# Moving the node numbers of the first edge stage's 0/1 matrices from SBUF into PSUM

## The chip, the core and the metric

The program runs on one core of a Trainium2 chip. The metric is the device time of one execution in microseconds (us). Three executions of the kernel before took 6554.74, 6558.20 and 6558.29 us, median 6558.2 us.

The engines are named as the profile names them: PE (TensorE matmul; PEld its weight loads), DVE (VectorE), ACT (ScalarE), POOL (GpSimd) and SP (SyncE, which issues DMAs here). SBUF is the working memory that all of them reach; PSUM holds the matmuls' outputs, in eight banks of 512 four-byte numbers per partition.

## The reference, cut to what matters

Two layers, each a graph attention followed by a mixture-of-experts feed-forward, over 6250 nodes with 256 features and 206250 edges sorted by their destination. The change lies in the attention of the first layer:

```
h = (x @ W.T).reshape(n, H, D)                        # H = 8 heads, D = 32
alpha = einsum(h[src], a_src) + einsum(h[dst], a_dst) + sum(relu(edge_attr @ edge_W.T + edge_b) * h[dst])
alpha = where(alpha >= 0, alpha, 0.2 * alpha)
ex = exp(alpha - segment_max(alpha, dst)[dst])
attn = ex / maximum(segment_sum(ex, dst)[dst], 1e-10)
out = segment_sum(h[src] * attn[..., None], dst) + bias
```

## The kernel before, in words

`edge_phase` runs once per layer. Edges go through it in groups of 512 (`G`), each group as 4 chunks (`CH`) of 128 edges on the 128 partitions. A group's destinations lie in a window of 32 nodes (`WIN`). Thirteen groups (`SB`) make a batch; 31 batches make a stage. Two batches stand in double buffers: `k` is 0 or 1 in `rows[:, k]`, `oh[:, k]`, `sel[:, k]` and `ps_w[:, k]`, where each `k` of `ps_w` is one PSUM bank. A loop body (`Fori`) holds two batches.

The engines work a batch in program order, tied by semaphores:

- POOL does nothing but `gather` (L774): 52 indirect DMAs per batch, each fetching the 128 source rows of a chunk from HBM by the numbers in `eidx`. Four gathers of batch b+2, slot s, may start when PE has finished slot s of batch b (`s_o`).
- PE, in slot s of batch b: `total` (L880, L886) sums the weighted rows of the 4 chunks into the window's 32 nodes, with the 0/1 matrix `oh` as weights, and carries the part that belongs to the window before with the 0/1 matrix `sel`. Between these it computes for batch b+2 the encodings (L809, L811) and scores (L821) of the edges. In slot 1 it adds the source logits of batch b+1 (`logits`, L851), which ACT copies out of the fetched rows (`sources`, L950) once all 52 gathers of that batch have landed; in slot 10 it writes batch b+1's transposed softmax weights into bank `1-k` of `ps_w` (L870), in columns 0 to 103 of each chunk's 128.
- ACT takes its work in this order: evict slot s (L973), the two ReLUs of batch b+2 (L946), and in slot 1 `sources` behind them.
- DVE scales the fetched rows by the weights (L1141), writes 0/1 matrices of owners (L1064), multiplies encodings (L1073), and once per batch does the maxima (L1094, L1099, L1103), a short chain on one partition (L1106 to L1118), `peaks` (L1122 to L1128) and, in slot 9, `one_hots` (L1085 and L1088).

`one_hots` for batch b+1 compares every edge's distance `dn` (SBUF, 52 numbers per partition) with the numbers 0 to 31 and so writes 52 x 32 = 1664 elements of `oh`; a second instruction does the same for `sel` (416 elements). In the first layer both tables of numbers lie in SBUF (`miota`, `pm`); in the second layer they are copied at the start into a PSUM bank of their own (`ps_i`), which the first layer has no room for.

At the stage's start DVE clears buffers and then increments `s_ready`; SP waits for that before it loads the first index tables, and POOL for the tables before its first gather.

Of the kernel before, what the change touches and what calls it, by code (L numbers as in the profile page):

```python
# [10 lines left out]
ALU = mybir.AluOpType  # L11
# [3 lines left out]
P = 128  # L15
# [8 lines left out]
CH = G // P  # L24
# [5 lines left out]
WIN = 32  # L30
K3 = 3 * WIN
SB = 13
COLS = SB * HEADS
# [33 lines left out]
def hold(eng, sem, value, passed):  # L67


    eng.wait_ge(sem, value)  # L70
    eng.sem_inc(passed, 1)
# [478 lines left out]
def edge_phase(nc, io, dr, layer):  # L550

    first = layer == 0
    with ExitStack() as ctx:
# [3 lines left out]
        OHW = SB * CH * WIN  # L557
# [10 lines left out]
        miota = sb("miota", [P, WIN], F32)  # L568
        pm = sb("pm", [P, WIN], F32)
# [3 lines left out]
        dn = sb("dn", [P, SB, CH], F32)  # L573
        dd = sb("dd", [P, SB], F32)
        oh = sb("oh", [P, 2, OHW + PAD_M], F32)
# [21 lines left out]
        if first:  # L597
            hp = sb("hp", [K3, RING, D], BF16)
            w_st = sb("w_st", [4, D], F32)
            w_rest = sb("w_rest", [4, D], F32)  # L600
            w_part = sb("w_part", [4, 3, D], BF16)
            w_enc = sb("w_enc", [K3, D], BF16)
            adst = sb("adst", [P, 2], F32)
            hmask = sb("hmask", [P, 2, HEADS], F32)
            hwide = sb("hwide", [P, 2, WIDE], F32)
            encr = sb("encr", [P, 2, G], F32)
            u = sb("u", [P, 2, 2, G], F32)
            lk, fmax, near = sb("lk", [COLS, G], F32), sb("fmax", [COLS, G], F32), mx
            nodes, lags = miota, pm
            ps_enc = ps("ps_enc", [P, 2, 512])  # L610
            ps_hd = ps("ps_hd", [P, 2, 512])
        else:
            aw = sb("aw", [K3, RING, WIDE], BF16)
            ps_k, ps_f, ps_i = ps("ps_k", [P, 512]), ps("ps_f", [P, 512]), ps("ps_i", [P, 512])
            lk, fmax, near = ps_k[0:COLS, :], ps_f[0:COLS, :], ps_f[0:COLS, :]
            nodes, lags = ps_i[:, 0:WIN], ps_i[:, WIN:2 * WIN]
        ps_X = ps("ps_X", [P, 512])
        ps_o = ps("ps_o", [P, OB, 512])
        ps_w = ps("ps_w", [P, 2, CH, P])
        small = lambda k: ps_w[:, k, :, :].rearrange("p j c -> p (j c)")  # L620
        s_nb, s_const, s_w, s_wp, s_we, s_init, s_ready = (sem(n) for n in ("nb", "const", "w", "wp", "we", "init", "ready"))
        s_ld = [sem(f"ld{r}") for r in range(RING)]
# [35 lines left out]
        def _(sp):  # L658
# [8 lines left out]
            def entry(t):  # L667
                why = "the planning stage writes only groups and starts of windows that lie inside their arrays"
                _, vals = nc.values_load_multi_w_load_instructions(tab[0:1, bass.ds(t * 3, 3)], engines=[sp.engine], min_val=0, max_val=NP,
                                                                   skip_runtime_bounds_check_because=why)  # L670
                return [nc.s_assert_within(x, 0, NG - 1 if c == 0 else NP, skip_runtime_bounds_check_because=why) for c, x in enumerate(vals)]
# [70 lines left out]
            for j in range(BEHIND):  # L742
                t = steps * (2 * SB) + (3 * SB + j)
                _, _, back = entry(t)
                store(t, j % SB, back)
# [270 lines left out]
        def _(v):  # L1016
            steps = [0]

            def done(ins):

                steps[0] += 1
                ins.then_inc(s_init, 1)
                v.wait_ge(s_init, steps[0])
# [13 lines left out]
            if first:  # L1037
                done(nc.vector.memset(hwide[:, :, :], 0.0))
                done(nc.vector.memset(w_enc[:, :], 0.0))
                done(nc.vector.tensor_copy(hwide[:, :, COLS - HEADS:COLS], hmask[:, :, :]))  # L1040
                v.sem_inc(s_ready, 1)
                v.wait_ge(s_w, 48)
                done(nc.vector.tensor_copy(w_part[:, 0, :], w_st[:, :]))
                done(nc.vector.tensor_tensor(w_rest[:, :], w_st[:, :], w_part[:, 0, :], ALU.subtract))
                done(nc.vector.tensor_copy(w_part[:, 1, :], w_rest[:, :]))
                done(nc.vector.tensor_tensor(w_rest[:, :], w_rest[:, :], w_part[:, 1, :], ALU.subtract))
                nc.vector.tensor_copy(w_part[:, 2, :], w_rest[:, :]).then_inc(s_wp, 1)
            else:
                done(nc.vector.memset(aw[:, :, :], 0.0))
                done(nc.vector.tensor_copy(nodes, miota[:, :]))  # L1050
                done(nc.vector.tensor_copy(lags, pm[:, :]))
                v.sem_inc(s_ready, 1)

# [28 lines left out]

            def one_hots(b, k):
                hold(v, s_dn, b * 2 + 2, s_pv)
                nc.vector.tensor_tensor(oh[:, k, 0:OHW].rearrange("p (x m) -> p x m", m=WIN),  # L1085
                                        dn[:, :, :].rearrange("p s j -> p (s j)").unsqueeze(2).to_broadcast([P, SB * CH, WIN]),
                                        nodes[:, :].unsqueeze(1).to_broadcast([P, SB * CH, WIN]), ALU.is_equal)
                nc.vector.tensor_tensor(sel[:, k, 0:SELW].rearrange("p (x m) -> p x m", m=WIN),  # L1088
                                        dd[:, :].unsqueeze(2).to_broadcast([P, SB, WIN]),
                                        lags[:, :].unsqueeze(1).to_broadcast([P, SB, WIN]), ALU.is_equal)  # L1090
# [54 lines left out]
            def phase(b, k, pre, turn, turns, next_turns):  # L1145
                m, n = b + 1, b + 2
                if pre:
                    node_ids(n, k, next_turns)
                if first and pre:
                    owners(n, k, 0, par(0))  # L1150
                carried(b, k)
                for s in range(SB):
                    if s + 2 < SB:
                        scaled(b, k, s + 2)
                    elif turn:
                        scaled(m, 1 - k, s + 2 - SB)
                    if pre and s + ahead < SB:
                        owners(n, k, s + ahead, par(s + ahead))
                    if first and pre:
                        products(n, s, par(s))  # L1160
                    if turn and s == 0:
                        distances(m, 1 - k, turns)
                    if turn and s == 1:
                        largest(m)
                    if turn and s == 2:
                        runs_forth(m, 1 - k, turns)
                    if turn and s == 3:
                        runs_back(m, 1 - k)
                    if turn and s == 5:
                        chain(m, 1 - k)  # L1170
                    if turn and s == 8:
                        peaks(m, 1 - k)
                    if turn and s == 9:
                        one_hots(m, 1 - k)
# [3 lines left out]
            for s in range(SB):  # L1178
                if s + 1 < SB:
                    owners(0, 0, s + 1, (s + 1) % 2)  # L1180
                if first:
                    products(0, s, s % 2)
            distances(0, 0, 0)
            one_hots(0, 0)
            largest(0)
            runs_forth(0, 0, 0)
# [600 lines left out]
def build(nc, io, out):  # L1787
    dr = scratch(nc)
    plan_phase(nc, io, dr)
    node_phase(nc, io, dr, 0)  # L1790
    edge_phase(nc, io, dr, 0)
    ffn_phases(nc, io, dr, 0, io["x"], dr["x2"], dr["x2"])
    node_phase(nc, io, dr, 1)
    edge_phase(nc, io, dr, 1)
    ffn_phases(nc, io, dr, 1, dr["x2"], dr["x3"], out)
# [22 lines left out]
```

## Time and profile before

| | |
|---|---|
| three executions | 6554.74, 6558.20, 6558.29 us |
| the profiled execution | 6560.36 us, span 6558.6 us (1.8 us lie outside the span) |
| PE busy | 4742.2 us, 72% of the span |
| POOL busy | 3639.3 us, 55% |
| DVE busy | 3265.5 us, 50% |
| ACT busy | 1360.8 us, 21% |
| first edge stage, first to last gather | 242.6 to 2341.3 us |
| second edge stage, first to last gather | 3739.3 to 5775.3 us |

Times count from the span's start. A row of the timeline gives the start, the duration, the engine, the line of the kernel, the operation, what it writes and reads, how many like it are merged, and in brackets how long the engine stood idle before it and what ended that. "issue" there is idle time that no semaphore explains. `e_` stands before the names of both edge stages. Matmuls are pipelined and their ends modelled, so PE's busy time says that work was in it, not that it ran at its peak.

### The profile page before, as it was taken

Reading aid. Unit: us, or ns where it says so; the run is one execution under the profiler, and the core shown is the slowest. Engines: PE = TensorE matmul, PEld = TensorE weight load, DVE = VectorE, ACT = ScalarE, POOL = GpSimd, SP = SyncE. Lnnn points to the kernel's source line nnn. Section 1 sums busy time; section 2 is a strip of 40 time slices with the busy share of each in tenths; the row PEclk is TensorE's granted clock in tenths of the full one; section 3 lists DMA queues with packets and bytes.
Section 4 is the critical chain, followed back from the end, with each engine's and each line's share of the span. In section 5 each row is a group of like instructions: output and inputs, shape, how many; then the busy total and the mean of one; then the engine's idle time right before and its main releaser. Section 6 shows DMA issues by size and latency. Waiting matters only on the chain. (4 is left out here: it accounts for less than half of the span.)

```text
span 6558.6 us, 98463 instructions
## 1 busy us (share of the span) xinstructions
PE 4742.2 (72%) x19729; PEld 3561.5 (54%) x19729; DVE 3265.5 (50%) x5938; ACT 1360.8 (21%) x2977; POOL 3639.3 (55%) x3708
## 2 busy tenths in 40 slices
PE   1699999999999963099999436565656565643798
PEld 0355555555555543099999325444544444433698
DVE  6666767767777757111111334444444444454344
ACT  1333333333333311022222201010101010101122
POOL 1677777777777720512222177777777777711322
PEclk9899999999999995599999668788888887875899
DMA  6566666666666634256666455555555555542455
GB/s 219 180 172 164 163 164 162 163 165 165 163 165 166 160 94 170 87 177 183 185 185 185 134 133 141 140 139 141 139 141 139 140 139 140 138 131 103 176 199 184
DMA packets 718012, 1022.22 MB, mean 156 GB/s; under 512 B 301733, under 2 KB 531561, under 8 KB 692608
## 3 DMA queue, kind: packets, MB, share of 16 engines
q0 software_dynamic: 183456, 485.95, 28.5%
q1 hardware_dynamic: 527676, 519.31, 25.9%
q10 hardware_dynamic: 6564, 14.14, 0.6%
q14 instruction: 287, 2.35, 0.1%
q8 instruction: 29, 0.48, 0.0%
HBM read 868.26 MB, written 153.27 MB: 156 GB/s over the span
## 5 line engine op out<-in xcount | busy, mean ns | idle before, releaser
L774 POOL DMA_INDIRECT e_rows<-sc_table,e_eidx x3224 | 3141.4, 974 | 1007.1 <-issue 932.1
L880 PE MATMUL e_ps_o<-e_rows,e_oh 128*128 128x264 f32 x6448 | 1633.5, 398 | 53.2 <-DVE e_rows L1141 26.9
L880 PEld LDWEIGHTS e_ps_o<-e_rows,e_oh 128*128 128x128 f32 x6448 | 1230.0, 195 | 412.8 <-issue 214.0
L1141 DVE TENSOR_TENSOR e_rows<-e_rows,e_ps_w 128x1024 f32<-128x1024 f32 x806 | 969.7, 1206 | 13.2 <-issue 9.6
L1073 DVE SCALAR_TENSOR_TENSOR e_u<-e_encr,e_adst,e_ps_hd 128x512 f32<-128x512 f32 x806 | 588.1, 743 | 470.8 <-PE e_ps_X L821 391.0
L821 PE MATMUL e_ps_X<-e_u,e_hwide 128*104 128x512 f32 x1612 | 806.3, 593 | 0.0
L973 ACT COPY e_res<-e_ps_o 32x264 f32<-32x264 f32 x806 | 296.4, 368 | 2131.1 <-PE e_ps_o L886 1689.5
L851 PE MATMUL e_ps_X<-e_ident,e_alog 128*104 128x128 f32 x496 | 97.9, 361 | 828.1 <-ACT e_alog L950 828.1
L1685 PE MATMUL x_ps_h<-x_xT,x_w 128*128 128x256 f32 x2624 | 647.2, 405 | 14.6 <-DMA x_b<-in_L_ffn_b_dram 14.6
L1685 PEld LDWEIGHTS x_ps_h<-x_xT,x_w 128*128 128x128 f32 x2624 | 638.0, 337 | 19.3 <-issue 15.5
L1696 PE MATMUL x_ps_y<-x_w,x_hT 128*128 128x256 f32 x2624 | 579.9, 379 | 0.0
L851 PEld LDWEIGHTS e_ps_X<-e_ident,e_alog 128*104 128x104 f32 x496 | 82.6, 234 | 854.9 <-issue 854.9
L1655 POOL DMA_INDIRECT sc_x<-x_y,x_idx x108 | 168.0, 1555 | 665.8 <-DVE x_idx L1729 649.2
L1696 PEld LDWEIGHTS x_ps_y<-x_w,x_hT 128*128 128x128 f32 x2624 | 492.9, 190 | 63.5
L946 ACT ACTIVATE e_encr<-e_ps_enc 128x512 f32<-128x512 f32 x806 | 468.9, 588 | 241.8 <-PE e_ps_enc L809 232.3
L1708 ACT ACTIVATE x_hT<-x_ps_h,x_b 128x256 f32<-128x256 f32 x656 | 305.4, 474 | 780.3 <-PE x_ps_h L1685 779.5
L886 PE MATMUL e_ps_o<-e_res,e_sel 128*128 128x264 f32 x1488 | 456.2, 389 | 0.0
L1064 DVE TENSOR_SCALAR e_ohT<-e_at,e_nid 96x512 bf16<-96x512 int16 x806 | 296.0, 368 | 319.9 <-DMA e_aw<-sc_a2p 213.7
L1094 DVE TENSOR_TENSOR e_ps_k<-e_ps_X,e_y 104x512 f32<-104x512 f32 x31 | 21.7, 699 | 820.8 <-ACT e_y L954 820.8
L821 PEld LDWEIGHTS e_ps_X<-e_u,e_hwide 128*104 128x104 f32 x1612 | 273.9, 170 | 179.5 <-issue 65.5
L1350 POOL DMA_INDIRECT sc_xb<-r_xt,r_slot_i x98 | 95.0, 969 | 437.2 <-DVEq L1555 407.9
L809 PE MATMUL e_ps_enc<-e_at,e_w_enc 96*128 96x512 bf16 x806 | 309.3, 384 | 38.8 <-DMA e_w_enc<-e_w_part 35.9
(290 smaller groups left out, 4066.7 us busy)
## 6 DMA issues: line engine op xcount, KB each, us to landing
x_w<-in_L_ffn_W_dram SPq DMA_DIRECT2D x112, 1024.0 KB
e_at<-sc_grp SPq DMA_DIRECT2D x403, 192.0 KB
x_w<-in_L_ffn_w_dram SPq DMA_DIRECT2D x60, 1024.0 KB
e_rows<-sc_table,e_eidx POOLq DMA_INDIRECT x3224
e_at<-sc_grp SPq DMA_DIRECT2D x403, 96.0 KB
sc_agg<-e_res SPq DMA_DIRECT2D x816, 33.0 KB
sc_xb<-r_zero SPq DMA_DIRECT2D x24, 1032.0 KB
x_xin<-sc_xb SPq DMA_DIRECT2D x86, 258.0 KB
```

What stands on the lines that cost most here:

```text
L774: pool.indirect_dma_start(rows[:, k, s, j, :], None, dr["table"][:, :], bass.IndirectOffsetOnAxis(eidx[:, k, s, j:j + 1], 0)).then_inc(s_r ...
L809: nc.tensor.matmul(ps_enc[:, h, :], w_enc[:, h * P:(h + 1) * P], at[:, ring(s), 0, :].bitcast(BF16), start=True, stop=True).then_inc(s_enc, 1)
L821: nc.tensor.matmul(ps_X[0:COLS, :], hwide[:, h, COLS - HEADS * (s + 1):2 * COLS - HEADS * (s + 1)], u[:, par(s), h, :], start=(s == 0 and ...
L880: nc.tensor.matmul(ps_o[:, q, 0:ROW], oh[:, k, at_j:at_j + P], rows[:, k, s, j, :], start=(j == 0), stop=False)
L886: nc.tensor.matmul(ps_o[:, q, 0:ROW], sel[:, k, s * WIN:s * WIN + P], seen, start=False, stop=True).then_inc(s_o, 1)
L946: nc.scalar.activation(encr[:, h, :], ps_enc[:, h, :], ACT.Relu).then_inc(s_relu, 1)
L973: nc.scalar.copy(res[0:WIN, kept(s), :], ps_o[0:WIN, par(s) % OB, 0:ROW]).then_inc(s_ev, 1)
L1073: nc.vector.scalar_tensor_tensor(u[:, p, h, :], encr[:, h, :], adst[:, h:h + 1], ps_hd[:, h, :], ALU.add, ALU.mult).then_inc(s_u, 1)
L1141: nc.vector.tensor_tensor(part, part, ps_w[:, k, :, s * HEADS:(s + 1) * HEADS].unsqueeze(3).to_broadcast([P, CH, HEADS, DH]), ALU.mult).th ...
L1685: mm = nc.tensor.matmul(ps_h[:, j % 4, 0:TB], w1[:, k, c, :].rearrange("p (m j) -> p j m", j=FC)[:, j, :], xT[:, k, c, :], start=(c == 0), ...
L1696: mm = nc.tensor.matmul(ps_y[:, s, 0:D], hT[:, k, j, s * P:(s + 1) * P], w2[:, k, j, :], start=(j == 0), stop=(j == FC - 1))
L1708: nc.scalar.activation(hT[:, k, j, :], ps_h[:, j % 4, 0:TB], ACT.Gelu if first else ACT.Relu, bias=b1[:, k, j:j + 1]).then_inc(s_act, 1)
```

## The change

The lag table `pm` stays where it was. The node numbers of the first layer get a second home: columns 104 to 119 of two of the four chunks of each `ps_w` bank, which the transposed weights (columns 0 to 103) and the small results in chunk 0 and chunk 3 leave alone. Sixteen numbers stand in each piece, so that both layers' comparison now walks its 32 columns as 2 x 16. For batch b+1 with buffer `1-k`, the numbers are read from bank `k`, the one that PE and ACT are not about to write for batch b+1. The second layer's table stays in `ps_i` and is only walked in the new way.

```
-            nodes, lags = miota, pm
+            lags = pm
...
-            nodes, lags = ps_i[:, 0:WIN], ps_i[:, WIN:2 * WIN]
+            lags = ps_i[:, WIN:2 * WIN]
...
+        HALF = WIN // 2
+        halves = lambda tile: tile.rearrange("p (a m) -> p a m", m=HALF)
+        nodes = (lambda k: ps_w[:, k, 1:3, COLS:COLS + HALF]) if first else (lambda k: halves(ps_i[:, 0:WIN]))
...
                 done(nc.vector.tensor_copy(hwide[:, :, COLS - HEADS:COLS], hmask[:, :, :]))
+                for k in range(2):
+                    done(nc.vector.tensor_copy(nodes(k), halves(miota[:, :])))
                 v.sem_inc(s_ready, 1)
...
-                done(nc.vector.tensor_copy(nodes, miota[:, :]))
+                done(nc.vector.tensor_copy(nodes(0), halves(miota[:, :])))
...
-                nc.vector.tensor_tensor(oh[:, k, 0:OHW].rearrange("p (x m) -> p x m", m=WIN),
-                                        dn[:, :, :].rearrange("p s j -> p (s j)").unsqueeze(2).to_broadcast([P, SB * CH, WIN]),
-                                        nodes[:, :].unsqueeze(1).to_broadcast([P, SB * CH, WIN]), ALU.is_equal)
+                nc.vector.tensor_tensor(oh[:, k, 0:OHW].rearrange("p (x a m) -> p x a m", a=2, m=HALF),
+                                        dn[:, :, :].rearrange("p s j -> p (s j)").unsqueeze(2).unsqueeze(3).to_broadcast([P, SB * CH, 2, HALF]),
+                                        nodes(1 - k).unsqueeze(1).to_broadcast([P, SB * CH, 2, HALF]), ALU.is_equal)
```

DVE's program at the start of the first edge stage before (`e_hwide` and `e_w_enc` are weights of the encoding, `e_w_st` and `e_w_part` its inputs being split):

```order
L1039 MEMSET e_w_enc 96x128
L1040 COPY e_hwide<-e_hmask 128x2x8
L1043 CAST e_w_part<-e_w_st 4x256
L1044 TENSOR_TENSOR e_w_rest<-e_w_st,e_w_part 4x256
L1045 CAST e_w_part<-e_w_rest 4x256
```

The same place in the changed kernel:

```order
L1042 MEMSET e_w_enc 96x128
L1043 COPY e_hwide<-e_hmask 128x2x8
L1045 COPY e_ps_w<-e_miota 128x2x16 x2
L1048 CAST e_w_part<-e_w_st 4x256
L1049 TENSOR_TENSOR e_w_rest<-e_w_st,e_w_part 4x256
```

Two copies have come in between the last copy and the increment of `s_ready`; nothing else moved on this engine.

DVE's program around the 0/1 matrices in the loop body before (L70 rows are register work of the waits):

```order
L1073 SCALAR_TENSOR_TENSOR e_u<-e_encr,e_adst,e_ps_hd 128x512
L1085 TENSOR_TENSOR e_oh<-e_dn,e_miota 128x1664
L1088 TENSOR_TENSOR e_sel<-e_dd,e_pm 128x416
L1141 TENSOR_TENSOR e_rows<-e_rows,e_ps_w 128x4x256
L70 ISA
L1064 TENSOR_SCALAR e_ohT<-e_at,e_nid 96x512
```

And in the changed kernel:

```order
L1078 SCALAR_TENSOR_TENSOR e_u<-e_encr,e_adst,e_ps_hd 128x512
L1090 TENSOR_TENSOR e_oh<-e_dn,e_ps_w 128x1664
L1093 TENSOR_TENSOR e_sel<-e_dd,e_pm 128x416
L1146 TENSOR_TENSOR e_rows<-e_rows,e_ps_w 128x4x256
L70 ISA
L1069 TENSOR_SCALAR e_ohT<-e_at,e_nid 96x512
```

The order is the same; the second input of the larger comparison is now `e_ps_w` instead of `e_miota`. The programs of PE, ACT, POOL and SP are as they were.

## Rows read from the trace of the kernel before

**Rows 1.** Windows: us, then busy of PE, PEld, DVE, ACT, POOL; clock; DMA; both stages.
```profile
242.60:2341.30 2098.70, 1989.79 (x7609) 1203.07 (x7610) 1450.64 (x2193) 639.33 (x1335) 1604.47 (x1612) 0.98 0.61 164
3739.00:5776.00 2037.00, 1121.71 (x4793) 877.43 (x4793) 884.82 (x1387) 212.22 (x530) 1536.93 (x1612) 0.79 0.55 139
```

**Rows 2.** Groups of POOL, first stage, then second.
```profile
L774 POOL DMA_INDIRECT e_rows<-sc_table,e_eidx x1612 | 1604.5, 995 | 500.8 <-issue 457.7 <-PE e_ps_o L886 36.5 <-DMA e_eidx<-sc_eslot 6.6
...
L774 POOL DMA_INDIRECT e_rows<-sc_table,e_eidx x1612 | 1536.9, 953 | 506.3 <-issue 474.4 <-PE e_ps_o L886 24.7 <-DMA e_eidx<-sc_eslot 7.3
```

**Rows 3.** Timeline, POOL and DVE around one pair of comparisons, first stage.
```profile
1034.29 2.26 POOL L774 DMA_INDIRECT e_rows<-sc_table,e_eidx  x1 [0.30 <-PE e_ps_o L886]
...
1033.35 1.88 DVE L1085 TENSOR_TENSOR e_oh<-e_dn,e_miota 128x1664 f32<-128x1664 f32 x1
1035.15 0.58 DVE L1088 TENSOR_TENSOR e_sel<-e_dd,e_pm 128x416 f32<-128x416 f32 x1
```

**Rows 4.** Timeline, the same place in the second stage.
```profile
4097.28 0.95 POOL L774 DMA_INDIRECT e_rows<-sc_table,e_eidx  x1 [0.30 <-issue]
...
4096.30 1.88 DVE L1085 TENSOR_TENSOR e_oh<-e_dn,e_ps_i 128x1664 f32<-128x1664 f32 x1
```

**Rows 5.** L1085: count, ns min/median/max, first and last start; by form.
```profile
L1085 DVE TENSOR_TENSOR e_oh<-e_dn,e_miota x31: 1874/1877/1892, 301.2 to 2368.7; 128x1664 f32<-128x1664 f32 x31
L1085 DVE TENSOR_TENSOR e_oh<-e_dn,e_ps_i x31: 1871/1877/1886, 3769.8 to 5799.6; 128x1664 f32<-128x1664 f32 x31
```

**Rows 6.** Groups of ACT from 445 to 2345 us: `sources`.
```profile
L950 ACT COPY e_alog<-e_rows 128x416 f32<-128x416 f32 x29 | 15.2, 523 | 2.8 <-DMA e_rows<-sc_table,e_eidx 2.8
```

**Rows 7.** Timeline, PE's `logits` in one batch, ACT's `sources` in another.
```profile
1057.77 1.09 PE L851 MATMUL e_ps_X<-e_ident,e_alog 128*104 128x128 f32 x8 [1.31 <-ACT e_alog L950]
...
1193.17 0.54 ACT L950 COPY e_alog<-e_rows 128x416 f32<-128x416 f32 x1 [1.32 <-DMA e_rows<-sc_table,e_eidx]
```

**Rows 8.** Timeline of PE behind two such waits, and the window of the first.
```profile
1194.78 3.63 PE L880 MATMUL e_ps_o<-e_rows,e_oh 128*128 128x264 f32 x8
...
1736.66 1.95 PE L880 MATMUL e_ps_o<-e_rows,e_oh 128*128 128x264 f32 x8
...
1194.82:1198.24 3.42, 3.42 (x10) 2.61 (x9) 2.08 (x3) 0.60 (x1) 2.51 (x4) 0.50 0.58 177
```

**Rows 9.** Timeline, DVE: the larger comparison of the next three batches.
```profile
1100.05 1.88 DVE L1085 TENSOR_TENSOR e_oh<-e_dn,e_miota 128x1664 f32<-128x1664 f32 x1
...
1168.00 1.88 DVE L1085 TENSOR_TENSOR e_oh<-e_dn,e_miota 128x1664 f32<-128x1664 f32 x1
...
1237.70 1.87 DVE L1085 TENSOR_TENSOR e_oh<-e_dn,e_miota 128x1664 f32<-128x1664 f32 x1
```

**Rows 10.** Timeline, the edge of the loop body: DVE and PE.
```profile
1117.93 0.23 DVE L1056 TENSOR_SCALAR e_nid<-e_ns,e_q 96x13 f32<-96x13 f32 x1 [3.65 <-issue]
...
1119.62 0.68 PE L886 MATMUL e_ps_o<-e_cs,e_sel 128*128 128x264 f32 x2 [1.01 <-DVE e_cs L1135]
```

**Rows 11.** Timeline, the stage's start: DVE, SP, POOL, ACT.
```profile
239.59 0.17 DVE L1040 COPY e_hwide<-e_hmask 128x16 f32<-128x16 f32 x1
...
239.85 0.40 SPq L675 DMA_DIRECT2D e_eidx<-sc_eslot  x1
...
302.06 1.82 POOL L774 DMA_INDIRECT e_rows<-sc_table,e_eidx  x1 [0.30 <-issue]
...
378.73 0.54 ACT L950 COPY e_alog<-e_rows 128x416 f32<-128x416 f32 x1 [3.71 <-DMA e_rows<-sc_table,e_eidx]
```

**Rows 12.** L1051, the second stage's table copy: count, ns, start.
```profile
L1051 DVE COPY e_ps_i<-e_pm x1: 195/195/195, 3736.2 to 3736.2; 128x32 f32<-128x32 f32 x1
```

**Rows 13.** L1108: count, ns min/median/max; timeline, POOL beside L1128, DVE behind a pair.
```profile
L1108 DVE COPY e_qrow<-e_ps_w x62: 514/524/534, 318.6 to 5788.6; 1x208 f32<-1x208 f32 x62
...
1030.29 1.19 POOL L774 DMA_INDIRECT e_rows<-sc_table,e_eidx  x1 [0.30 <-issue]
...
1040.86 0.75 DVE L1073 SCALAR_TENSOR_TENSOR e_u<-e_encr,e_adst,e_ps_hd 128x512 f32<-128x512 f32 x1 [1.03 <-PE e_ps_X L821]
```

## The prediction

> **What bounds the kernel now.** I read four views of the first edge stage, since the change acts only there: the windows, the groups of POOL, the timeline around one pair of comparisons, and who ends ACT's and PE's waits.
>
> The windows show a stage of 2098.70 us between first and last gather, with matmuls in 1989.79 us of it and POOL busy for 1604.47 us [rows 1]. The groups of POOL show that the rest of POOL's time is not waiting for anybody: 1612 gathers of 995 ns with about 0.30 us between them [rows 2]. Busy plus idle is 1604.5 + 500.8 = 2105.3 us, the whole stage and the wait before its first gather. So POOL runs back to back, 2098.7 / 31 = 67.70 us per batch, and looks like the bound.
>
> It is slowed in this stage. A gather that comes up against DVE's two comparisons takes 2.26 us instead of 0.95 [rows 3]: the comparison starts at 1033.35, the smaller one ends at 1035.73, and the gather ends 0.82 us later. In the second stage the same comparison, with its second input in PSUM, runs over a gather of 0.95 us [rows 4], and the mean gather there is 953 ns against 995 [rows 2]. The two stages differ by 1604.5 - 1536.9 = 67.6 us of POOL time; the pair of comparisons accounts for (2.26 - 0.95) x 30 = 39 us of it.
>
> But who waits for POOL? ACT's `sources` needs all 52 gathers of a batch. From 445 us to the end of the stage, 29 batches, ACT stood idle for them 2.8 us in all [rows 6]. In a usual batch ACT goes from its ReLUs straight to the copy, and PE waits 1.31 us for that chain [rows 7], which no gather shortens. Between one comparison and the next lie 66.70 us (1033.35 to 1100.05), then 67.95 us [rows 3, 9]. The longer ones hold the loop's edge, where DVE is idle 3.65 us with no cause that a semaphore shows and PE waits 1.01 us for DVE's carried sums [rows 10]. So PE sets the pace, and POOL keeps up with almost nothing to spare.
>
> **The larger comparison.** 31 instructions in each stage, 1664 elements as before. Its duration with the second input in PSUM is in the trace: 1877 ns median, against 1877 with both inputs in SBUF [rows 5]. What no row shows is runs of 16 numbers with a gap between them. From below I take no gain. From above I take the PSUM copy with short runs, 208 elements in 524 ns [rows 13], against the table copy, 32 elements in 195 ns [rows 12]: 329 / 176 = 1.87 ns per element, where the two comparisons cost (1877 - 580) / (1664 - 416) = 1.04 ns [rows 3, 5]. That would add 0.83 x 1664 = 1.4 us. I take 0, because the same instruction is the nearest row. If it came, 1.03 us of it lie beside idle DVE time, for behind the pair DVE next waits 1.03 us for PE [rows 13].
>
> The Trainium skill (VectorE: DVE Perf Modes, section on the TRN2 errata) gives a VectorE operation from PSUM a fixed 120 cycles where one from SBUF has 58, 62 cycles at 0.96 GHz or 0.065 us. By that, an estimate from the page, the stage's comparisons would cost 31 x 0.065 = 2.0 us more on DVE; by the two equal medians [rows 5] they cost nothing, and the measurement decides.
>
> **POOL's stall.** Removed: the part of the 1.31 us that the larger comparison causes. Left: the smaller one, 0.58 us with both inputs in SBUF [rows 3]. Its residue is between 0 (a gather is past its start) and 0.58 us; I take 0.24, from the gather of 1.19 us beside the subtraction L1128, which also has two inputs in SBUF and ends the batch's `peaks` [rows 13]. So POOL saves 1.31 - 0.24 = 1.07 us per batch, between 0.73 and 1.31, and its pace becomes 67.70 - 1.07 = 66.6 us, below PE's mean, which is (66.70 + 67.95) / 2 = 67.3 us for the pair shown. POOL then runs ahead until it waits for `s_o`; that wait holds nobody, since the gathers are a batch and more ahead of their use.
>
> **What this gives the stage.** Only where somebody waited for gathers.
> 1. The three waits of 1.32, 0.92 and 0.53 us that make up the 2.8 us: -2.8 us [rows 6, 7].
> 2. Behind the first of them the clock is granted at half for 3.42 us, at 0.50 that is 1.2 GHz, after PE had stood idle; eight matmuls took 3.63 us there and 1.95 in the batch of the second wait [rows 8]. The batch took 1237.70 - 1168.00 = 69.70 us; less 66.70, less the 1.4 us of wait, 1.6 us remain for the clock: -1.6 us. Bounds 0 (the low clock comes elsewhere) and -1.7 from the matmuls.
> 3. The start. ACT waited 3.71 us for batch 1's gathers at 378.73 [rows 11], so everything behind follows POOL there. The gather beside the first comparison took 1.82 us, 0.87 too long, with some 0.1 left to the smaller comparison: -0.8 us.
> 4. Added: two table copies, each waited for, between L1040 and `s_ready`. SP issues the index table 0.09 us behind L1040's end, so it waited for DVE [rows 11]. The second stage's copy takes 0.195 us and its neighbour starts 0.23 us earlier, so 2 x 0.23 = +0.5 us, bounds 0.3 and 0.6.
>
> The sum is -2.8 - 1.6 - 0.8 + 0.5 = -4.7 us. Against the profiled execution: 6560.4 - 4.7 = 6555.7 us. That execution was 2.2 us above the median of the three runs, 6558.2, so I forecast 6553.5 us.
>
> The second stage: POOL is as busy as before, its comparison never held a gather, and the new walk through the same table is the question bounded above. DVE is busy 884.82 of 2037 us there [rows 1], which hides 31 x 1.4 us too. I take 0. After the stage nothing is changed.
>
> **Rivals.**
> A. POOL sets the pace. For it: POOL never pauses, and its 67.70 us equal the stage's own pace. Then all of the relief arrives: 30 x 1.07 + 0.8 - 0.5 = 32 us, or 6526 us; with the full 1.31 us, 39 us. Against it: 2.8 us of waiting in 29 batches, and a batch of 66.70 us while POOL needs 67.70 on average. What speaks for a part of it is that POOL drops back until it causes a wait now and then; that part is in my sum.
>
> B. The stall stays, because it hangs on something else than two inputs in SBUF (the table's place is not what holds the gather, or the smaller comparison holds it all). Only the copies remain: +0.5, or 6558.7 us. Against it stands the second stage, where the gather under the comparison took 0.95 us [rows 4]. The Trainium skill (SBUF — State Buffer, section on its two separate sides) says that a VectorE operation with two SBUF inputs and a GpSimd operation exclude each other for a whole instruction; by that rule, the trace agrees that the larger comparison stops holding gathers and the smaller one does not.
>
> C. Slower: the walk in runs of 16 from PSUM lengthens the comparison, and DVE's slack behind it is not there. It sits at L1085's place in both stages. With 1.4 us per batch and 1.03 covered it costs 31 x 0.37 = 11 us; with nothing covered 31 x 1.4 = 43 us, less the 4.7 gained: 6597 us. It decides from about 1.6 us of added length where the cover holds, since (1.6 - 1.03) x 31 = 18 us outweighs the 4.7 by 13. Against it: L1085's equal medians, and DVE's 1450.64 us of 2098.70.
>
> **How the numbers follow.** Forecast 0.79, A 0.12, B 0.05, C 0.04. The forecast's own range is 6548 to 6560 us: nothing gained and the copies paid at the top with a run at the high end, and at the bottom the full sum, the low clocks of two more batches saved (1.6 us each, as behind the first wait), and a run at the low end of the three. For 8 in 10 with A and C outside, the range is 6544 to 6561 us. Within 0.2% of 6558.2, about 13 us and roughly what a measurement of this kernel can tell from no change, lie the forecast and B; with the edges of the forecast that makes 0.83 for no change, 0.13 for faster (A), 0.04 for slower (C).
>
> **What the profile would show.** Right: L1090 with `e_ps_w` at 1.88 us; no gather of 2.26 us, the longest beside the smaller comparison under 1.6 us; POOL busy near 1604.5 - 33 = 1571 us in the stage, with idle time now ended by PE's sums; `sources` waiting for gathers under 1 us behind the first two batches; most distances between comparisons still 66.70 us, those at the loop's edge unchanged. Wrong: distances below 66.5 us (A); gathers still of 2.26 us (B); L1090 above 2.9 us, or PE waiting for DVE in slots 10 and 11 (C). The forecast also fails if the waits at the loop's edge turn out to hang on the gathers, which I have taken as DVE's own.

## The result, and the profile after

The changed kernel is slower: 6580.4 us, median of 6 runs (6574.7 to 6586.7), against 6555.7 us for the kernel before in the same series (6 runs, 6546.7 to 6558.3). The ratio is 1.0039, with a 95% interval of 1.0028 to 1.0050. The forecast was 6553.5 us with 6561 as its upper end, and slower had a chance of 4%. The prediction was wrong.

| profiled execution | before | after |
|---|---|---|
| span | 6558.6 us | 6572.6 us |
| first gather of the first stage | 242.6 us | 244.6 us |
| first edge stage, first to last gather | 2098.7 us | 2117.0 us |
| between the stages | 1398.0 us | 1399.2 us |
| second edge stage | 2036.0 us | 2027.2 us |
| behind it | 783.3 us | 784.6 us |

The loss of 18.3 us stands in the first edge stage, the one that the change was to relieve. (The second stage of the kernel before was some 8 us slow in this one profiled execution, with gathers of 953 ns; in eleven of the twelve other kernels profiled here it took 2026 to 2029 us, with gathers of some 950 ns. Compared by medians the change costs 24.7 us, by profiled executions only 14: beside those 8 us, the profiled execution after, 6574.8 us, is at the low end of its six.)

The two windows after, with the columns of [rows 1] (us, then busy time of PE, PEld, DVE, ACT, POOL, granted clock, DMA share):

```profile
244.60:2361.60 2117.00, 1995.91 (x7604) 1205.95 (x7604) 1448.61 (x2193) 639.64 (x1335) 1558.45 (x1612) 0.98 0.61 162
3760.00:5788.10 2028.10, 1119.66 (x4793) 876.24 (x4793) 883.91 (x1387) 212.16 (x530) 1530.52 (x1612) 0.79 0.56 140
```

POOL is busy 46.0 us less than in [rows 1], more than the 33 us forecast, DVE's busy time has hardly moved (2.0 us less), and PE's has grown by 6.1 us with no more matmuls. So the stage became longer by waiting, for the most part. The group of POOL answers to [rows 2], the timeline beside a pair of comparisons to [rows 3], and the group of ACT's `sources`, from 446 us on, to [rows 6]:

```profile
L777 POOL DMA_INDIRECT e_rows<-sc_table,e_eidx x1612 | 1558.5, 967 | 565.6 <-issue 454.7 <-PE e_ps_o L889 103.8 <-DMA e_eidx<-sc_eslot 7.1
```

```profile
1248.18 0.95 POOL L777 DMA_INDIRECT e_rows<-sc_table,e_eidx  x1 [0.30 <-PE e_ps_o L889]
1249.43 1.01 POOL L777 DMA_INDIRECT e_rows<-sc_table,e_eidx  x1 [0.30 <-issue]
...
1247.24 1.87 DVE L1090 TENSOR_TENSOR e_oh<-e_dn,e_ps_w 128x1664 f32<-128x1664 f32 x1
1249.04 0.57 DVE L1093 TENSOR_TENSOR e_sel<-e_dd,e_pm 128x416 f32<-128x416 f32 x1
```

```profile
L953 ACT COPY e_alog<-e_rows 128x416 f32<-128x416 f32 x29 | 15.1, 521 | 0.0
```

The gather under the comparison takes 0.95 us where it took 2.26, and the next one, beside the smaller comparison, 1.01. Of 1612 gathers 29 were over 2 us before and none is after; the mean has gone from 995 to 967 ns, POOL waits 103.8 us for PE instead of 36.5, and ACT waits for no gather at all. And the comparison that reads PSUM in runs of 16 is no longer than before [rows 5]:

```profile
L1090 DVE TENSOR_TENSOR e_oh<-e_dn,e_ps_w x31: 1868/1872/1889, 304.2 to 2389.7; 128x1664 f32<-128x1664 f32 x31
```

The change did what it says. What became late instead is in PE's waits in the stage (columns: total us, times, longest), here for the kernel before and then for the changed one:

```profile
PE e_ps_X L851 <- ACT e_alog L950: 39.2, 28, 2.7
PE e_ps_o L886 <- DVE e_cs L1135: 18.9, 13, 2.3
```

```profile
PE e_ps_X L854 <- ACT e_alog L953: 40.9, 29, 4.2
PE e_ps_o L889 <- DVE e_cs L1140: 36.1, 13, 3.7
```

PE waits for the carried sums `e_cs` 13 times in either kernel, once at each edge of the loop body, but for 36.1 us instead of 18.9, or 1.32 us longer each time. The distances from one larger comparison to the next say the same: over the 14 even batches from the third on they add up to 937.9 us before and 933.9 after (all at 66.7 after), over the 13 batches with an edge in them to 892.6 and 917.5. So the even batches gained 4.0 us, the 13 edges lost 24.9.

The timeline of DVE and PE at one edge, before (columns: start, duration, engine, line; the idle time ahead and its releaser in brackets):

```profile
1255.52 0.23 DVE L1056 TENSOR_SCALAR e_nid<-e_ns,e_q 96x13 f32<-96x13 f32 x1 [3.58 <-issue]
1256.31 0.39 DVE L1064 TENSOR_SCALAR e_ohT<-e_at,e_nid 96x512 bf16<-96x512 int16 x1 [0.56 <-DVE e_nid L1056]
1256.62 0.40 DVE L1133 TENSOR_TENSOR e_cs<-e_res,e_ps_w 32x256 f32<-32x256 f32 x1
1256.95 0.14 DVE L1135 TENSOR_TENSOR e_cs<-e_res,e_ps_w 32x8 f32<-32x8 f32 x1
1258.02 1.22 DVE L1141 TENSOR_TENSOR e_rows<-e_rows,e_ps_w 128x1024 f32<-128x1024 f32 x1 [0.93 <-issue]
...
1257.23 0.68 PE L886 MATMUL e_ps_o<-e_cs,e_sel 128*128 128x264 f32 x2 [0.98 <-DVE e_cs L1135]
```

And the same edge after:

```profile
1265.31 0.23 DVE L1061 TENSOR_SCALAR e_nid<-e_ns,e_q 96x13 f32<-96x13 f32 x1 [3.83 <-issue]
1266.10 0.35 DVE L1069 TENSOR_SCALAR e_ohT<-e_at,e_nid 96x512 bf16<-96x512 int16 x1 [0.56 <-DVE e_nid L1061]
1267.77 0.41 DVE L1138 TENSOR_TENSOR e_cs<-e_res,e_ps_w 32x256 f32<-32x256 f32 x1 [1.32 <-issue]
1268.11 0.14 DVE L1140 TENSOR_TENSOR e_cs<-e_res,e_ps_w 32x8 f32<-32x8 f32 x1
1268.18 1.20 DVE L1146 TENSOR_TENSOR e_rows<-e_rows,e_ps_w 128x1024 f32<-128x1024 f32 x1
...
1268.39 0.68 PE L889 MATMUL e_ps_o<-e_cs,e_sel 128*128 128x264 f32 x2 [2.60 <-DVE e_cs L1140]
```

DVE halts twice behind the loop's branch in both kernels, and no semaphore ends either halt. The first, of about 4 us, is in the same place. The second stood ahead of L1141, which PE does not wait for at once; it now stands two instructions earlier, ahead of the carried sums, which PE does wait for. Over all 13 edges the groups of DVE give 9.6 us of it before and 19.7 after, 0.74 and 1.52 us an edge (columns as in [rows 6]; before, then after):

```profile
L1141 DVE TENSOR_TENSOR e_rows<-e_rows,e_ps_w 128x1024 f32<-128x1024 f32 x377 | 454.9, 1207 | 9.6 <-issue 9.6
L1138 DVE TENSOR_TENSOR e_cs<-e_res,e_ps_w 32x256 f32<-32x256 f32 x29 | 11.8, 408 | 19.7 <-issue 19.7
```

Counted in the trace with waits and register work, before, the 15th instruction behind the branch meets the second halt, after, the 13th. Two is the number of copies that the change adds to DVE's program, ahead of the loop.

What a longer wait can do to the clock stands at another edge after, in the timeline of PE and the windows of its wait and of what follows:

```profile
1130.62 1.10 PE L889 MATMUL e_ps_o<-e_cs,e_sel 128*128 128x264 f32 x2 [2.42 <-DVE e_cs L1140]
```

```profile
1128.20:1130.60 2.40, 0.00 (x0) 0.01 (x1) 0.95 (x4) 0.00 (x0) 0.95 (x1) 1.00 0.41 113
1130.62:1134.00 3.38, 3.38 (x8) 1.90 (x9) 1.95 (x3) 1.48 (x3) 1.17 (x2) 0.52 0.01 2
```

PE did nothing for 2.4 us, and the 3.38 us behind that ran at a granted clock of 0.52, near the lower level of 1.2 GHz: the same two matmuls took 1.10 us, and 0.68 in the fence above, where a wait of 2.60 us was followed by no such stretch. So the length of one wait does not decide it, but longer waits meet it more often: between 380 and 2330 us there are 7 such stretches after (23.9 us in all), all of them at edges, and 3 before (10.2 us), two of them at edges and the third the one of [rows 8]. At 1.6 us each, the price read from that one in the prediction's second term, four more make 6 us, as much as PE's busy time grew. For the edges alone it is five more, an estimated 8 us, and these with the 17.2 us of longer waits make the 24.9 that the edges lost.

### The profile page after: what moved, and what is told of

It is laid out like the page before. It is cut to its first block and busy times, and to the rows that moved or that the text cites. A ratio compares the mean times of both kernels' runs of the same rounds, so it can differ in the third digit from the quotient of the medians.

```text
span 6572.6 us, 98465 instructions
## 1 busy us (share of the span) xinstructions
PE 4747.4 (72%) x19729; PEld 3564.3 (54%) x19729; DVE 3263.7 (50%) x5940; ACT 1361.0 (21%) x2977; POOL 3585.9 (55%) x3708
## 5 line engine op out<-in xcount | busy, mean ns | idle before, releaser
L777 POOL DMA_INDIRECT e_rows<-sc_table,e_eidx x3224 | 3089.0, 958 | 1069.7 <-issue 925.5
L1690 PEld LDWEIGHTS x_ps_h<-x_xT,x_w 128*128 128x128 f32 x2624 | 637.6, 337 | 19.1 <-issue 15.6
```

The costliest lines, as they stand in the source:

```text
L777: pool.indirect_dma_start(rows[:, k, s, j, :], None, dr["table"][:, :], bass.IndirectOffsetOnAxis(eidx[:, k, s, j:j + 1], 0)).then_inc(s_r ...
L1690: mm = nc.tensor.matmul(ps_h[:, j % 4, 0:TB], w1[:, k, c, :].rearrange("p (m j) -> p j m", j=FC)[:, j, :], xT[:, k, c, :], start=(c == 0), ...
```

## The experiments

The theory: DVE gets its program in pieces. The branch at the loop's edge makes it fetch a piece (first halt), and where that piece ends soon behind the branch's target (the instruction that the branch goes to) it halts again for the next (second halt). Adding instructions ahead of the loop moves the places where pieces end, and two moved the second halt ahead of the carried sums. The rival: the way of the change itself costs the time at the edge, by DVE's reads of the other batch's PSUM bank, or by gathers that now come at other moments. In each series the kernels ran on one chip, with runs of the kernel before beside them; its medians there were 6552.6 us (for the first four kernels of the table), 6549.3 (the next four) and 6550.6 us (the last three). The last two columns come from the one profiled execution of each; there the kernel before has 2098.7 and 18.9 us and the changed kernel 2117.0 and 36.1.

| kernel | median us | ratio to before, interval | first stage us | PE's waits for `e_cs` us |
|---|---|---|---|---|
| pad2_only | 6583.05 | 1.0046 (1.0032 to 1.0059) | 2124.8 | 34.7 |
| psum_unshifted | 6546.43 | 0.9991 (0.9982 to 1.0000) | 2094.7 | 17.9 |
| before_pad13 | 6616.97 | 1.0097 (1.0082 to 1.0113) | 2160.9 | 64.9 |
| before_pad14 | 6579.27 | 1.0041 (1.0027 to 1.0054) | 2115.7 | 34.5 |
| psum_early60 | 6545.65 | 0.9994 (0.9984 to 1.0003) | 2091.4 | 18.3 |
| psum_early100 | 6539.97 | 0.9984 (0.9975 to 0.9994) | 2090.6 | 17.3 |
| psum_early117 | 6542.08 | 0.9991 (0.9981 to 1.0000) | 2087.4 | 16.8 |
| before_early100 | 6550.39 | 1.0001 (0.9991 to 1.0011) | 2100.4 | 15.6 |
| after_early98 | 6545.49 | 0.9996 (0.9987 to 1.0005) | 2085.9 | 15.6 |
| after_carried | 6567.28 | 1.0025 (1.0015 to 1.0035) | 2122.3 | 6.4 |
| psum_early100_carried | 6535.55 | 0.9976 (0.9966 to 0.9986) | 2083.7 | 3.5 |

### The two copies without the change

Into the kernel before, behind L1040; nobody reads what they write:

```diff
+for k in range(2):
+    done(nc.vector.tensor_copy(ps_w[:, k, 1:3, COLS:COLS + WIN // 2], miota[:, :].rearrange("p (a m) -> p a m", m=WIN // 2)))
```

> The kernel before with the two copies of the change added at DVE's start and never read; the comparison still reads its node numbers from SBUF in runs of 32. Theory (place of the code): the two added instructions move everything behind them in DVE's program by two places, so that DVE's second halt at the loop's edge comes ahead of the carried sums (L1133) instead of behind them. Then this kernel is slow too: PE's waits for the carried sums in the first stage add up to 34 to 38 us instead of 18.9, the stage grows by 15 to 20 us, and the time is 6570 to 6580 us. Rival 1 (the PSUM table): reading the numbers from the weights' banks or in runs of 16 costs the time; then this kernel takes 6556 us, within 4. Rival 2 (POOL ahead): gathers that run ahead of PE lengthen DVE's halt at the edge; then too 6556 us, since POOL is held as before here.

It took 6583.05 us, 30.4 above the kernel before and as much as the changed kernel, with its 29 gathers of over 2 us still there. The expectation was 3 us short. The edge is that of the changed kernel:

```profile
1269.36 0.23 DVE L1058 TENSOR_SCALAR e_nid<-e_ns,e_q 96x13 f32<-96x13 f32 x1 [4.11 <-issue]
...
1271.54 0.41 DVE L1135 TENSOR_TENSOR e_cs<-e_res,e_ps_w 32x256 f32<-32x256 f32 x1 [0.82 <-issue]
```

Its waits of PE:

```profile
PE e_ps_o L886 <- DVE e_cs L1137: 34.7, 13, 3.8
```

The whole loss comes with two copies that have nothing to do with the comparison, while the comparison still reads SBUF and the gathers are held as before, so both forms of the rival fall.

### The change without two more instructions

In the changed kernel, one copy for both banks and one clear where there were two, so that DVE's program is as long as before:

```diff
-for k in range(2):
-    done(nc.vector.tensor_copy(nodes(k), halves(miota[:, :])))
+done(nc.vector.tensor_copy(ps_w[:, :, 1:3, COLS:COLS + HALF], halves(miota[:, :]).unsqueeze(1).to_broadcast([P, 2, 2, HALF])))
...
+if first:
+    nc.vector.memset(oh[:, :, OHW:OHW + PAD_M], 0.0)
...
-nc.vector.memset(oh[:, k, OHW:OHW + PAD_M], 0.0)
+if not first:
+    nc.vector.memset(oh[:, k, OHW:OHW + PAD_M], 0.0)
```

> The change whole, but with DVE's program kept at its old length: both banks are filled by one copy, and the clearing of two buffers' ends (L1031) is one instruction instead of two, so everything behind stands where it stood in the kernel before. Theory (place of the code): PE's waits for the carried sums fall back to 17 to 21 us, no gather is over 2 us, and the time is the one first forecast, 6546 to 6554 us, about 5 under before. Rivals 1 and 2 (PSUM table; POOL ahead): as slow as the changed kernel, 6575 to 6585 us.

It took 6546.43 us, 6.2 below the kernel before, inside the expected range. PE's waits for the carried sums are back to 17.9 us, and ACT's for gathers stay at nothing. So the loss is gone once the change does not move the program, and what is left agrees with the 4.7 us of the prediction's sum, though the interval (0 to 12 us) would also admit nothing.

### The end of a piece moved on purpose

Clears of one unused number each, behind L1047 of the kernel before: 13 should let the first piece end just behind the target of the branch, 14 should let a piece begin there.

```diff
+for i in range(13):   # 14 in the other kernel
+    nc.vector.memset(spare[0:1, i:i + 1], 0.0)
```

> The kernel before with 13 clears of one unused number each behind L1047, where DVE waits for a table anyway. Theory (place of the code): 14 of DVE's instructions behind the loop's branch come with the first piece of code now, so with 13 more ahead only one does, and DVE halts a second time ahead of L1056. The carried sums then come about 1.3 us later than in the changed kernel: PE waits for them about 4 us per edge, 52 us in all, and the time is 6585 to 6605 us. Rivals: padding does nothing beyond its 13 x 0.1 us beside a wait, 6556 us.

> As the one with 13, but 14 clears. Theory (place of the code): the first instruction behind the branch is now the first of its piece, so a whole piece is there after the first halt and the second halt disappears: no idle time without a cause ahead of L1141 at the edge, PE waits for the carried sums 15 to 20 us in all, and the time is 6545 to 6556 us, a cliff of 30 us or more against 13 clears. Rivals: no difference between 13 and 14.

With 13 the time is 6616.97 us, 64 above the kernel before and 12 above the expected range, with 64.9 us of waits where 52 were expected; with one clear more it falls by 38 us. The timeline of one edge with 13:

```profile
1285.02 0.23 DVE L1059 TENSOR_SCALAR e_nid<-e_ns,e_q 96x13 f32<-96x13 f32 x1 [7.38 <-issue]
```

Both halts stand one behind the other ahead of L1059. The page's row on the queue of instructions (packets, MB, share), with 13 clears and then before:

```profile
q14 instruction: 300, 2.46, 0.1%
```

```profile
q14 instruction: 287, 2.35, 0.1%
```

Thirteen packets more for thirteen edges, of some 8 KB each (0.11 MB / 13): one fetch more at each edge. The groups of DVE at the first instruction behind the branch (columns as in [rows 6]), with 14 clears and then before:

```profile
L1059 DVE TENSOR_SCALAR e_nid<-e_ns,e_q 96x13 f32<-96x13 f32 x28 | 6.9, 247 | 63.2 <-issue 63.2
```

```profile
L1056 DVE TENSOR_SCALAR e_nid<-e_ns,e_q 96x13 f32<-96x13 f32 x28 | 9.9, 354 | 52.2 <-issue 52.2
```

With 14 the second halt is gone, as expected, but the first is 63.2 / 13 = 4.86 us and not 52.2 / 13 = 4.02, and that was not: the expected 6545 to 6556 us were missed by 23.

The packets of q14 themselves, timed in the traces, show what ends the halts. In the kernel before, at each of the 13 edges one packet lands 2.8 us behind the branch on average and a second at 5.5; DVE's first instruction starts 1.5 to 1.7 us after the first of them, and L1141, behind the second halt, 1.3 to 1.5 us after the second. In the changed kernel the carried sums start 1.1 to 1.5 us after the second. With 13 and with 14 clears two packets stand close together (2.4 and 3.5 us behind the branch with 13, 2.6 and 3.6 with 14), and DVE starts only 1.6 to 1.7 us after the later one. That is the longer first halt, and with 13 a part of the excess over the expectation. Why the engine needs two packets there stays open.

### Long first pieces

If a first piece ends far behind the target, the next has come by then. In `psum_unshifted` and in the kernel before, n clears of an unused number at the end of DVE's part of the planning stage, far ahead of the edge stage:

```diff
+for i in range(100):   # 60 and 117 in the other kernels
+    nc.vector.memset(spare[0:1, i:i + 1], 0.0)
```

> The same with 60 clears: 82 instructions come with the first piece. Theory (place of the code): no halt near the edge but the first; 6538 to 6552 us if that is 4.0 us, 6560 to 6570 if it is 4.9. Rival: 6546.

> The same with 100 clears: 42 instructions behind the branch come with the first piece. Theory (place of the code): as with 117, 6538 to 6552 us if the first halt stays at 4.0 us, 6560 to 6570 if it is 4.9. Rival: 6546.

> The change whole on DVE's old length (one copy for both banks, one clear merged), and 117 clears of one unused number each at the end of the planning stage, where DVE waits 32 us at a barrier. If a piece of DVE's code holds 128 instructions, 25 of them behind the loop's branch now come with the first piece instead of 14. Theory (place of the code): the second halt at the edge moves behind instruction 25, where DVE has other work or is late anyway, so the halt ahead of L1141 (0.8 us per edge) goes; PE's waits for the carried sums stay near 18 us, or rise towards 35 us if the first halt grows by 0.9 us as it did with the branch's target at a piece's start. Time 6538 to 6552 us in the first case, 6560 to 6570 in the second. Rival (only the number of clears right ahead of the stage matters): 6546, as without them.

> The kernel before (numbers in SBUF) with the 100 clears. Theory (place of the code): the change's own worth is the same at every place, 4 to 8 us, so this is 4 to 8 us slower than psum_early100. Rival (the worth hangs on the place): outside that.

The three of the changed way (`psum_early60`, `psum_early100`, `psum_early117`) are inside their expected ranges and within 6 us of each other, at 6545.65, 6539.97 and 6542.08 us. They lie 3.7 to 9.4 us below their series' kernel before, where `psum_unshifted` lay 6.2 below its own: taking the second halt away from L1141 has gained nothing that these runs tell apart, so the rival on record for them is not excluded. The edge in `psum_early100` has one halt only:

```profile
1249.33 0.23 DVE L1066 TENSOR_SCALAR e_nid<-e_ns,e_q 96x13 f32<-96x13 f32 x1 [3.87 <-issue]
1250.79 1.20 DVE L1151 TENSOR_TENSOR e_rows<-e_rows,e_ps_w 128x1024 f32<-128x1024 f32 x1
```

The packets at the edges move with the clears. By 128 instructions to a piece, 14 of those behind the branch are in the first piece before, and 25, 42 and 82 with 117, 100 and 60 clears. The third packet behind the branch lands 8.1 us behind it in the kernel before, 10.4 with 117 clears and 13.5 with 100, and with 60 none comes within 16 us; it is asked for when 19 instructions have started in the kernel before, 38 or 39 with 117 clears, 49 or 50 with 100, and 91 to 95 with 60. Pieces of 256 would place the three ends at 153, 170 and 210, which does not fit.

The kernel before gains nothing from the same 100 clears, 6550.39 us against 6549.34, although PE's waits at its edges fall to 15.6 us. In its trace ACT's waits for gathers have grown from 2.8 to 6.3 us: with shorter edges POOL is late in four batches, which is a part of rival A. With both at the same place the change is worth 6550.39 - 6539.97 = 10.4 us, more than the 4 to 8 expected. So the rival of that expectation came: what the change is worth hangs on the place, since shorter edges leave POOL less time.

### The changed kernel itself, with its pieces moved back

The changed kernel word for word, with 98 such clears (98 and its two more instructions make 100):

> The changed kernel word for word, with 98 clears of one unused number each at the end of the planning stage. Its DVE code is 2 instructions longer than the old one, so with 98 more it stands as in psum_early100: 42 instructions behind the branch in the first piece. Theory (place of the code is all): PE's waits for the carried sums fall from 36 to 16 to 19 us and the time is that of psum_early100 within 4 us, 6536 to 6545 us. Rival (the two separate copies or the two clears cost something themselves): over 6550 us.

It took 6545.49 us (11 runs) against 6550.62, half a microsecond above the expected range, where the changed kernel had taken 6580.4 against 6555.7 in its own series. The low clock is granted nowhere between 380 and 2330 us, and PE's waits for the carried sums are 15.6 us. Useless work far away took away the whole loss.

### The carried sums first

Another remedy is to let PE's input come ahead of the second halt:

```diff
+if first:
+    carried(b, k)
...
-carried(b, k)
+if not first:
+    carried(b, k)
```

> The changed kernel with one edit more: in the first layer DVE makes the carried sums (L1138, L1140) first thing in a batch, ahead of the node numbers and the owners (L1061, L1069). Theory (PE waits for the carried sums at the edge, and the second halt came ahead of them): they now come with the first piece of code, about 0.8 us earlier than even in the kernel before; PE's waits for them fall to under 12 us, but the owners stand behind the second halt, and PE needs them for its next encodings, so part comes back there. Time 6545 to 6570 us. If only the sums matter, 6535 to 6545. Rival: no effect, 6580.

> psum_early100 with the carried sums first. No second halt is near, so both gains add: the sums come 0.8 to 1.1 us earlier per edge, PE's waits for them fall from 17 to 3 to 8 us, part of it back in a wait for the owners. Theory: 6528 to 6538 us. Rival (POOL's pace of 66.4 us, or the ReLU chain, takes the rest back): 6538 to 6542 us.

In the changed kernel it gives back a third, inside the expected range: 6567.28 us, 16.7 above the kernel before in its series where the change alone was 24.7 above. PE's waits of the stage show why it is no more: the 0/1 matrices of owners, `e_ohT`, now come behind the halt, and PE waits for them:

```profile
PE e_ps_enc L812 <- DVE e_ohT L1069: 26.1, 13, 2.3
PE e_ps_o L889 <- DVE e_cs L1140: 6.4, 11, 1.0
```

Together with the long first piece there is one halt, and both waits are small:

```profile
PE e_ps_enc L815 <- DVE e_ohT L1074: 8.3, 13, 0.8
PE e_ps_o L892 <- DVE e_cs L1145: 3.5, 9, 1.1
```

At 6535.55 us, as expected, this version beats both kernels, the one before by 0.24% (interval 0.14 to 0.34%).

## Why the prediction was wrong

**What failed: term 4, the added copies at +0.5 us.** I read in the order that "nothing else moved on this engine" and priced two instructions by the 0.23 us that each takes. Their own time was right. The first gather came 1.9 us later, of which 1.4 stand ahead of the copies already (L1043 at 240.98, where L1040 started at 239.59 in [rows 11]; over the 13 kernels profiled that copy starts anywhere from 237.9 to 241.7 us), leaving 0.5. From that copy to the first gather lie 3.0 to 3.1 us in the four kernels without added copies and 3.5 to 3.6 in the four with two. What I left out is where they put everything behind them in DVE's program. In [rows 10] the halt of 3.65 us with no cause stood in front of me, I took it as given and did not ask what ends it, nor look at the next DVE instructions, where L1141 had a second one. `pad2_only` gave that term on its own: +30.4 us instead of +0.5. What stood in its place is a fetch: two instructions more in DVE's program put the second halt ahead of the carried sums, and PE waited 36.1 us for them instead of 18.9.

**Terms 1 and 2 were right.** The waits of `sources` are gone, and the even batches all take 66.7 us, the 69.70 of one of them with the low clock included; they gained 4.0 us against the 4.4 of both terms. Term 3 cannot be told apart: from the first larger comparison to the second lie 121.9 us before and 119.5 after, but 119.5 to 123.1 in the other kernels with the numbers in PSUM. `psum_unshifted` puts the sum of the relief, with one added copy, at 6.2 us, with an interval from 0 to 12.

**The comparison's length** was right at no change, 1872 ns against 1877. The extra fixed cost of PSUM that the Trainium skill states (VectorE: DVE Perf Modes, on the TRN2 errata) does not show in these rows either.

**POOL.** Busy 1558 us against my 1571. The residue beside the smaller comparison is 0.06 us (1.01 - 0.95) in nearly every batch, where I took 0.24 from another instruction. That is a matter of when the gather starts: 0.39 us into that comparison of 0.57, so that only 0.18 us of it could have held the gather. The comparisons' share of POOL's time went from 39 us to under 2; the other 9 of the 46 us saved come from gathers beside DVE's other instructions, its maxima above all, and no term of mine had them. That gathers held back almost nobody was right for the kernel as it stood, and for that alone: `before_early100` shows POOL one step behind PE.

**The rivals.** A did not come, since PE still set the pace, B did not, since the gather is 0.95 us, and C did not by its own mechanism, since no DVE instruction became longer. The forecast's sentence on what would show it wrong, the distances at the loop's edge "unchanged", is the one that broke: their mean went from 68.66 to 70.58 us. It broke by DVE's own halt and not by the gathers.

Rival C, the only one on the slow side, was built from the change's own operation. None of the rivals asked what adding instructions does in itself, though the halt behind a branch was in the rows. The first halt is one that the Trainium skill states: Runtime: NRT & Kernel Launch, in the section on instruction fetch mechanics, says that a taken branch to a target outside the fetched window makes the engine wait until the target's page has come by DMA. The trace agrees, with 4 us at each edge. The second stage fits it too: its loop body has 227 of DVE's instructions, waits and register work counted, where that of the first has 515, and behind its branch the next instruction starts after 0.2 us.

**What stays open.** Why two packets are needed at once where a piece starts at the target or just behind it. By how much the kernel before scatters by itself: its medians in four series went from 6549.3 to 6555.7 us. And what makes the 5.7 us between `psum_early60` and `psum_early100`, ten runs of each in one series, with only one halt near the edge in both.

## What to carry to other kernels

Where an engine halts behind a loop's branch, as DVE did here behind a body of 515 instructions and not behind one of 227, every instruction added to or taken from its program ahead of the loop moves the place of a second halt, and such a move can cost more than the change gives. Before pricing an edit, look at the idle times without a releaser behind the branch, see which instruction stands behind each and who waits for it, and count how far the edit moves them. To judge an idea apart from this, measure it with the program's length kept, and the padding alone beside it.

## What the runs showed of the hardware

- Behind the branch of the first stage's loop DVE halts about 4.0 us (means of 3.78 to 4.15 in eleven kernels, 4.86 in the one with 14 clears), and again for 0.7 to 1.5 us where the piece ends 12 to 14 instructions behind the branch. It starts again 1.0 to 1.7 us after an instruction packet has landed. Behind the branch of the second stage's loop, with a body of 227 instructions instead of 515, it does not halt. At two instructions' move the whole kernel went from 6552.6 to 6583.1 us, at thirteen to 6617.0.
- DVE's instructions come by q14 in packets of 8 KB (thirteen more with thirteen more fetches); all positions seen fit 128 instructions to a piece. The packets of q8, 29 with 0.48 MB in all, are of 16 KB.
- A DVE comparison with one input in PSUM does not hold a gather at all (0.95 us); one with both in SBUF, and the smaller one behind it, made it 2.26. The Trainium skill (SBUF — State Buffer, on the two separate sides) states the rule, for a GpSimd operation that reads SBUF. The smaller comparison, both inputs in SBUF, lengthened by 0.06 us a gather that started 0.18 us before its end.
- Reading PSUM in runs of 16 numbers with a gap costs nothing: 1872 ns for 1664 numbers.
- With PE's waits at the edges at 2.2 to 3.7 us, 7 of 13 were followed by 3.4 us at half the clock; with 0.7 to 2.3 us it was 2 of 13. So waits that grow can cost more than their length: 24.9 us at the edges for 17.2 us of waiting.
